# Folding an attention block's output projection into a router and the first expert matrices, and running a split matmul as one contraction

## The reference

```python
def _forward(hs, q_w, ..., o_w, o_b, router_w, router_b, w1, b1, w2, b2):
    Q = (hs @ q_w + q_b).reshape(B, S, H, HD).transpose(0, 2, 1, 3)        # H = 16
    K = (hs @ k_w + k_b).reshape(B, S, H, KPH).transpose(0, 2, 1, 3)       # KPH = 4
    V = (hs @ v_w + v_b).reshape(B, S, H, KPH).transpose(0, 2, 1, 3)
    scores = jnp.einsum('bhsk,bhtk->bhst', Q[..., :KPH], K) / math.sqrt(KPH)
    ao = jnp.einsum('bhst,bhtv->bhsv', jax.nn.softmax(scores, axis=-1), V)
    ao = ao.transpose(0, 2, 1, 3).reshape(B, S, H * KPH)                   # 64 features
    ao = jnp.concatenate([ao, jnp.zeros((B, S, D - LAT))], axis=-1)
    mla_out = ao @ o_w + o_b
    probs = jax.nn.softmax(mla_out @ router_w + router_b, axis=-1)
    topw, topi = jax.lax.top_k(probs, 2)
    combine = ...                                                          # 8 weights per token
    h1 = jnp.einsum('bsd,edf->ebsf', mla_out, w1) + b1[:, None, None, :]   # 8 experts, 256 wide
    h1 = jax.nn.gelu(h1, approximate=False)
    h2 = jnp.einsum('ebsf,efd->ebsd', h1, w2) + b2[:, None, None, :]
    return hs + 0.3 * jnp.einsum('bse,ebsd->bsd', combine, h2)

x = x + _L0_xattn_ref(_layernorm(x), ctx_1024)      # attention over 77 context rows
x = x + _L0_ffn_ref(_layernorm(x), ...)             # the block above
x = x + _L1_xattn_ref(_layernorm(x), ctx_1024, ...) # a second one over the context
x = x + _L1_ffn_ref(_layernorm(x), ...)             # one expert of 512
```

## Time and profile before

| | us |
|---|---|
| median of 3 runs | 174.09 |
| lowest and highest | 173.69, 174.84 |
| profiled execution | 173.32 |
| its span in the profile | 171.5 |
| PE busy in the span | 156.5 |
| mean granted clock of PE | 0.988 |

### The profile page before, as it was taken

One profiled execution on the slowest core, in us unless ns is written; L12 is line 12 of the kernel. 1 busy time (PEld: TensorE's weight loads), 2 busy tenths in 40 slices (PEclk: granted clock), 3 DMA queues, 4 the chain that ended last, 5 costly groups with the idle time before them and its releaser, 6 DMA issues.

```text
span 171.5 us, 4032 instructions
## 1 busy us (share of the span) xinstructions
PE 156.5 (91%) x1358; PEld 127.3 (74%) x1366; DVE 107.4 (63%) x401; ACT 106.5 (62%) x234; POOL 41.5 (24%) x122
## 2 busy tenths in 40 slices
...
GB/s 111 126 13 258 234 26 71 94 25 160 135 196 70 4 0 4 0 4 2 2 4 0 0 0 0 4 0 0 4 2 0 0 4 2 0 4 0 0 63 61
DMA packets 10527, 7.21 MB, mean 42 GB/s; under 512 B 1596, under 2 KB 9868, under 8 KB 10508
## 3 DMA queue, kind: packets, MB, share of 16 engines
...
## 4 chain that ended last, share of the span: by engine, by line
issue 53%; PE 22%; DVE 10%; POOL 5%; DMA 3%; ACT 3%; SPq 1%; ACTq 1%; POOLq 1%; DVEq 0%
PE ps L1012 20%; DVE nmax L820 4%; DMA qbd<-scratch_q 3%; POOL rstd L534 2%; DVE qbd L814 2%; POOL xn L528 2%; PE ps L1034 1%; DVE res L789 1%; DVE part L792 1%; DVE part L789 1%; SPq L383 1%; ACTq L55 1%; ACT part L601 1%; SPq L384 1%; ACT pexp L620 1%
## 5 line engine op out<-in xcount | busy, mean ns | idle before, releaser
L657 ACT ACTIVATE vpad<-ps,cols 128x256 f32<-128x256 f32 (+1 forms) x48 | 23.9, 543 | 23.8 <-PE ps L1012 23.7
L1012 PE MATMUL ps<-w2s,vpad 128*128 128x128 f32 x256 | 32.1, 277 | 0.0
L1012 PEld LDWEIGHTS ps<-w2s,vpad 128*128 128x128 f32 x256 | 30.3, 192 | 0.6 <-issue 0.2
L909 DVE SCALAR_TENSOR_TENSOR vpad<-ps,comb,vpad 128x128 f32<-128x128 f32 x64 | 18.6, 343 | 15.5 <-PE ps L1012 15.5
L820 DVE TENSOR_REDUCE nmax<-ps 128x4 f32<-128x512 f32 x32 | 21.0, 685 | 4.1 <-PE ps L1012 4.1
L620 ACT ACTIVATE pexp<-ps 128x512 f32<-128x512 f32 x32 | 18.6, 597 | 5.5 <-PE ps L1012 3.5
L1012 PE MATMUL ps<-mla_hi,w_lo 128*128 128x256 f32 (+1 forms) x48 | 17.7, 370 | 0.2 <-ACT vpad L657 0.2
L1012 PE MATMUL ps<-kst,qbd 128*128 128x128 bf16 x128 | 12.1, 225 | 5.0 <-DVE qbd L814 2.4
L1012 PEld LDWEIGHTS ps<-kst,qbd 128*128 128x128 bf16 x128 | 8.4, 101 | 10.0 <-issue 7.9
L528 POOL TENSOR_TENSOR xn<-vpad,bqv 128x256 f32<-128x256 f32 (+1 forms) x3 | 2.7, 909 | 53.0 <-DVE vpad L909 53.0
L1012 PE MATMUL ps<-mla_hi,w_hi 128*128 128x256 f32 (+1 forms) x48 | 15.3, 319 | 0.0
...
## 6 DMA issues: line engine op xcount, KB each, us to landing
...
```

Of the source, the lines that this page charges most:

```text
L657: act.activation(hT[:, k % 2, c, 0:n], ps[:, h1_bank(k, c), 0:n], ACT.Gelu, bias=cols[:, e * F0 + c:e * F0 + c + 1]).then_inc(s["gelu_ok"], 1)
L909: dve.scalar_tensor_tensor(out=x2[:, a + i, :], in0=ps[:, 2 + k % 2, i * D:(i + 1) * D], scalar=comb[:, a + i, e:e + 1], in1=x2[:, a + i, ...
L1012: return nc.tensor.matmul(dst, lhsT, rhs, start=start, stop=stop)
```

## The change

`oproj` goes. The output weights are transposed on PE once (`oT`: ACT writes `woT`, each lane of 32 rows holding 16 rows of -wo and 16 of +wo) and multiplied into the router weights (`fr`: `rwo`, `rbo`) and into `w1` of each expert (`fold:e`: one 256-wide fp32 matmul and two of one column for the bias, copied back by ACT over `w1s`; `fb` adds the biases on DVE). POOL's split of `w1` now waits for its fold. `den` is two matmuls: `selnum` brings the numerators into both halves of each lane, so that `aoT` holds the attention output twice per lane. ACT rounds it to `ao_hi`, and DVE forms `ao2`, which is -high in the rows of the negative weights and the low part in the others (`ao2 = aoT * lower - ao_hi`). With that, `m1` needs two matmuls per chunk instead of three. `comb_T` uses a transpose, one record, in place of an fp32 matmul with the identity. `wo` comes by one transfer of 64 rows instead of four. Several semaphores are merged. In bank 4, `fold`, `oT` and `fr` take turns with `den` and the router. The whole text of the order is rewritten; of its 35 lines the first is shown. The warm-up matmuls are 35 instead of 54.

```diff
-        wo = sb("wo", [P, D])
-        mla_hi = sb("mla_hi", [D, NHALF, T], FP32R)
-        mla_lo = sb("mla_lo", [D, NHALF, T], FP32R)
+        wo = sb("wo", [LAT, D])
+        woT = sb("woT", [D, LANES, 2, GROUPS, KPH])
+        lower = sb("lower", [P, 1])
+        ao_hi = sb("ao_hi", [D, NHALF, T], FP32R)
+        ao2 = sb("ao2", [D, NHALF, T], FP32R)
...
-        w1s = sb("w1s", [D, E0, F0 * P])
+        w1s = sb("w1s", [P, E0, F0 * P + F0])
...
-            warm:13 a_v:0 selg z_mask p1_stats:0 p1_norm:0 z_sel:0 z_v:0 warm:4 a_v:1 p1_ctx:0 warm:1 p1_T:0 warm:5 p1_stats:1
+            warm:1 selg a_v:0 warm:1 a_v:1 warm:1 z_mask warm:4 z_v:0 warm:5 z_q:0 z_den warm:2 p1_stats:0 a_q:0 warm:1 p1_norm:0
...
             def split_w1(e):
-                if e == 0:
-                    pool.wait_ge(s["w1_in"], 48)
-                a = did(pool.tensor_copy(w1_hi[:, e, :], w1s[:, e, :]))
-                after(a)
-                pool.tensor_tensor(out=w1_lo[:, e, :], in0=w1s[:, e, :], in1=w1_hi[:, e, :].bitcast(FP32),
+                w = w1s[:, e, 0:F0 * P]
+                pool.wait_ge(s["w1o_ok"], e + 1)
+                a = did(pool.tensor_copy(w1_hi[:, e, :], w))
+                after(a)
+                pool.tensor_tensor(out=w1_lo[:, e, :], in0=w, in1=w1_hi[:, e, :].bitcast(FP32),
                                    op=ALU.subtract).then_inc(s["w1_split"], 1)
...
-            def oproj(h):
-                act.wait_ge(s["o_ps"], h + 1)
-                act.activation(mlaT[:, h, :], ps[:, 4, :], ACT.Identity, bias=cols[:, R_OB:R_OB + 1]).then_inc(s["mla_ok"], 1)
-                act.wait_ge(s["mla_ok"], h + 1)
-                act.activation(mla_hi[:, h, :], mlaT[:, h, :], ACT.Copy).then_inc(s["mlahi_ok"], 1)
+            def high_part(h):
+                act.wait_ge(s["ao_ok"], HALF * (h + 1))
+                act.activation(ao_hi[:, h, :], aoT[:, h, :], ACT.Copy).then_inc(s["aohi_ok"], 1)
+
+            def wo_T():
+                act.wait_ge(s["woT_ps"], 1)
+                v = ps[:, 4, 0:LAT].rearrange("p (g j v) -> p j g v", g=GROUPS, v=KPH)
+                act.activation(woT[:, :, 0], v, ACT.Copy, scale=-1.0)
+                act.activation(woT[:, :, 1], v, ACT.Copy).then_inc(s["woT_ok"], 1)
+
+            def fold(e):
+                act.wait_ge(s["w1o_ps"], e + 1)
+                act.activation(w1s[:, e, :], ps[:, 4, 0:F0 * P + F0], ACT.Copy).then_inc(s["w1o_ok"], 1)
...
-                                   bias=cols[:, e * F0 + c:e * F0 + c + 1]).then_inc(s["gelu_ok"], 1)
+                                   bias=b1o[:, e, c:c + 1]).then_inc(s["gelu_ok"], 1)
...
-                dve.tensor_tensor(out=aoT[:, h, i * S:(i + 1) * S], in0=un[:, b % 2, :], in1=rden[:, b % 2, :],
+                dve.tensor_tensor(out=aoT[:, h, i * S:(i + 1) * S], in0=ps[:, 4, S:2 * S], in1=rden[:, b % 2, :],
                                   op=ALU.mult).then_inc(s["ao_ok"], 1)
 
-            def oproj(h):
-                dve.wait_ge(s["mlahi_ok"], h + 1)
-                dve.tensor_tensor(out=mla_lo[:, h, :], in0=mlaT[:, h, :], in1=mla_hi[:, h, :].bitcast(FP32),
-                                  op=ALU.subtract).then_inc(s["mlalo_ok"], 1)
+            def low_part(h):
+
+                dve.wait_ge(s["aohi_ok"], h + 1)
+                dve.wait_ge(s["obs_ok"], 2)
+                dve.scalar_tensor_tensor(out=ao2[:, h, :], in0=aoT[:, h, :], scalar=lower[:, 0:1], in1=ao_hi[:, h, :].bitcast(FP32),
+                                         op0=ALU.mult, op1=ALU.subtract).then_inc(s["ao2_ok"], 1)
+
+            def wo_T():
+                dve.wait_ge(s["cols_ok"], 1)
+                dve.tensor_scalar(obs[:, :], ones[:, :], cols[:, R_OB:R_OB + 1], None, ALU.mult).then_inc(s["obs_ok"], 1)
+                dve.wait_ge(s["ident_ok"], 1)
+                dve.tensor_reduce(lower[:, :], ident[:, :].rearrange("p (j x) -> p j x", j=LANES)[:, :, 16:32], axis=AX.XY,
+                                  op=ALU.add).then_inc(s["obs_ok"], 1)
+
+            def router_fold():
+
+                dve.wait_ge(s["rwo_ps"], 1)
+                dve.wait_ge(s["obs_ok"], 2)
+                dve.tensor_scalar(rwo[:, :], ps[:, 4, 0:E0], lower[:, 0:1], None, ALU.mult)
+                dve.tensor_tensor(out=rbo[:, :], in0=ps[:, 4, E0:2 * E0], in1=rb[:, :], op=ALU.add).then_inc(s["rwo_ok"], 1)
+
+            def bias_fold():
+                dve.wait_ge(s["w1o_ok"], E0)
+                dve.wait_ge(s["cols_ok"], 1)
+                dve.tensor_tensor(out=b1o[:, :, :], in0=w1s[:, :, F0 * P:F0 * P + F0],
+                                  in1=cols[:, 0:E0 * F0].rearrange("p (e c) -> p e c", c=F0), op=ALU.add).then_inc(s["b1o_ok"], 1)
...
-                pe.wait_ge(s["ln_ok"] if b else s["part_ok"], b or NFRONT)
-                if b >= HALF:
-                    pe.wait_ge(s["mla_ok"], 1)
-                if b >= HALF + 1:
+                pe.wait_ge(s["ao_ok"] if b else s["rwo_ok"], b or 1)
+                if 1 <= b <= HALF:
+                    pe.wait_ge(s["w1o_ok"], 2 * b)
+                elif b > HALF:
                     pe.wait_ge(s["lg_sub"], 1)
-                mm(ps[:, 4, 0:S], selden[:, :], un[:, b % 2, :]).then_inc(s["den_ps"], 1)
-
-            def oproj(h):
-                pe.wait_ge(s["ao_ok"], HALF * (h + 1))
-                pe.wait_ge(s["ow_in"], 16 * LANES)
-                mm(ps[:, 4, :], wo[:, :], aoT[:, h, :]).then_inc(s["o_ps"], 1)
+                mm(ps[:, 4, 0:S], selden[:, :], un[:, b % 2, :])
+                mm(ps[:, 4, S:2 * S], selnum[:, :], un[:, b % 2, :]).then_inc(s["den_ps"], 1)
+
+            def wo_T():
+                pe.wait_ge(s["w1_in"], 64)
+                pe.wait_ge(s["part_ok"], NFRONT)
+                nc.tensor.transpose(ps[:, 4, 0:LAT], wo[:, :], ident[0:LAT, 0:LAT]).then_inc(s["woT_ps"], 1)
+
+            def router_fold():
+
+                pe.wait_ge(s["woT_ok"], 1)
+                pe.wait_ge(s["obs_ok"], 1)
+                mm(ps[:, 4, 0:E0], woT[:, :, :, :, :].rearrange("p j a g v -> p (j a g v)"), rw[:, :])
+                mm(ps[:, 4, E0:2 * E0], obs[:, :], rw[:, :]).then_inc(s["rwo_ps"], 1)
+
+            def fold(e):
+
+                if e % 2:
+                    pe.wait_ge(s["w1o_ok"], e)
+                else:
+                    pe.wait_ge(s["ao_ok"], e // 2 + 1)
+                n = F0 * P
+                mm(ps[:, 4, 0:n], woT[:, :, :, :, :].rearrange("p j a g v -> p (j a g v)"), w1s[:, e, 0:n])
+                for c in range(F0):
+                    last = mm(ps[:, 4, n + c:n + c + 1], w1s[:, e, c * P:(c + 1) * P], cols[:, R_OB:R_OB + 1])
+                last.then_inc(s["w1o_ps"], 1)
 
             def router(h):
-                pe.wait_ge(s["mla_ok"], h + 1)
-                if h == 0:
-                    pe.wait_ge(s["ln_ok"], HALF + 1)
-                pe.wait_ge(s["w1_in"], 48)
+                pe.wait_ge(s["ao_ok"], BATCH if h else HALF + 1)
                 for n in range(HALF):
-                    last = mm(ps[:, 4, n * E0:(n + 1) * E0], mlaT[:, h, n * S:(n + 1) * S], rw[:, :])
+                    last = mm(ps[:, 4, n * E0:(n + 1) * E0], aoT[:, h, n * S:(n + 1) * S], rwo[:, :])
...
-                    last = mm(ps[0:E0, (7, 4)[h], n * S:(n + 1) * S], comb[:, h * HALF + n, :], ident[:, :])
+                    last = nc.tensor.transpose(ps[0:E0, (7, 4)[h], n * S:(n + 1) * S], comb[:, h * HALF + n, :], ident[:, :])
...
-                split3(ps[:, h1_bank(k, c), 0:n], w1_hi[:, e, f], w1_lo[:, e, f], x4_hi[:, toks(u)], x4_lo[:, toks(u)]).then_inc(s["h1_ps"], 1)
+                dst, x = ps[:, h1_bank(k, c), 0:n], ao2[:, :, :].rearrange("p h t -> p (h t)")[:, toks(u)]
+                mm(dst, w1_lo[:, e, f], x, True, False)
+                mm(dst, w1_hi[:, e, f], x, False, True).then_inc(s["h1_ps"], 1)
```

More of the change, by code:

```diff
@@ L100, in build @@
         aoT = sb("aoT", [P, NHALF, T])
-        mlaT = sb("mlaT", [D, NHALF, T])
+        own = sb("own", [P, NHALF, T])
         VB = GROUPS * LANES * ROWS
@@ L297, in build @@
-            s2:6,1 s2:6,2 un:5 av:5,3 w1:3 av:6,0 p4_ctx:0 combine:0 mT:7 s2:6,3 den:5 p4_ctx:1 s2:7,0 s2:7,1 msp:4 av:6,1 av:6,2
-            norm:4 norm:5 un:6 av:6,3 cT:0 av:7,0 s2:7,2 norm:6 s2:7,3 msp:5 norm:7 den:6 b2:0 av:7,1 av:7,2 w1:4 un:7 av:7,3
-            m1:0,0,0 msp:6 den:7 x2_init:0 gelu:0,0 m1:0,0,1 m1:0,1,0 oproj:1 m1:0,1,1 m1:0,2,0 gelu:0,1 gelu:0,2 m1:0,2,1
-            router:1 gelu:0,3 m2:0,0 m2:0,1 m1:0,3,0 m1:0,3,1 acc:0,0 m1:0,4,0 m2:0,2 gelu:0,4 gelu:0,5 acc:0,1 m1:0,4,1 cT:1 w1:5
```

118 lines of the change are left out of this document (62 added, 56 removed).

## The result

The changed kernel takes 167.54 us in the median of four runs (167.11 to 168.65), the kernel before 173.89 beside it; the ratio is 0.9637 with an interval of 0.9576 to 0.9699. Medians here are of all runs, while a ratio leaves out runs more than 1.5% above the fastest of their kernel. The profiled execution took 167.53 us for its span of 165.7.

The account below looks back on a forecast made before the run. PE's matmuls bound the kernel after 60 us, the query reload and DVE's maxima before. -5.1 + 0.8 + 0.5 = -3.8, plus 0.2 makes -3.6: 169.7 profiled, 170.5 us median, range 166.5 to 174.8.

Parts of the forecast that it names:

- 1.6 hidden: Between score groups of batches 4 and 5: 1.6 us of PE's added work is covered beside DVE's maxima.
- The third matmul, 7.4 us, of which 0.8 is lost: Expert stage: dropping each `m1` chunk's third matmul saves PE 7.4 us; 0.8 of 8 is charged for DVE or latency.
- The work that comes before the first `m1`: Behind the reload: five folds (4.25 us), `selnum` (1.2) and moved softmax and `av` groups (1.1), together 6.55 on PE.
- Before the reload, +0.5: Ahead of the second half's first score group: PE's extra 2.35 us delays it by up to 1 us, costing 0.5.
- 0.2 us charged for `msp:6`: POOL's maxima split for batch 6 queues behind `w1` splits and may be up to 1 us late; 0.2 added.
- Warm-up matmuls at nothing: Front: fewer warm-ups may bring a second half-clock window, but DVE binds there; 0 to 1 us, taken as 0.
- Rival B: Folds cost their whole 6.8 us and DVE or the PE-gelu chain binds late: -1.0, 173 us; chance 0.25.
- Rival D: Attention: PSUM bank 4, shared by `den`, folds, router and `oT`, sets the pace: +2, 176.1 us; chance 0.14.
- its own sign of more than 7 us between two `den` calls: Attention: if bank 4 sets the pace, the changed profile shows `den` calls more than 7 us apart.
- its other sign: Attention: if bank 4 sets the pace, PE idles before a `den` or a fold, released by ACT's copy.
- Rival C: Everything added is covered, by openings before the reload and maxima after it; only removals count: -6.5, 167.6 us; chance 0.15.

Follow-up runs that it names:

- a_three: The changed kernel with a third matmul put back into every `m1` chunk; 175.14 us, ratio 1.0071 to the kernel before.
- b_two: The kernel before with one of three matmuls per `m1` chunk left out, in the old order; ratio 0.9814 to the kernel before.
- b_aq3: The kernel before with ACT's zeroing of the last query tile moved earlier in the order; 174.04 us, ratio 1.0006.
- b_aq3w1: The kernel before with ACT's zeroing earlier and POOL's first `w1` split behind the maxima's split of sequence 2; 172.90 us, ratio 0.9943.
- a_again: The changed kernel run once more, unaltered, on the same chip as a repeat with more warm-up matmuls; 168.04 us.
- b_two_ct: The kernel before with two matmuls per `m1` chunk and the second half's combine-weight transpose moved behind `m1:0,5,1`; 170.33 us, ratio 0.9806.
- a_nofold: The changed kernel with all eight folds of `w1`, ACT's copies and their waits left out; 167.25 us, ratio 0.9554.

## Why the prediction was nearly right, and where it was not

The forecast was 170.5, the result 167.54, inside the range (166.5 to 174.8) but with a gain of 6.3 us where I had 3.6. In the profiled executions it is 5.8 (173.32 to 167.53); 0.6 more comes from the kernel before, whose profile was one of its shorter runs. The time fell in the range, and PE's busy time fell by 3.6 us (2.5 to 4 forecast), but the other sizes that the prediction names for the trace mostly did not come out: first score group of sequence 4 at 50.58 (51.3 to 52 forecast), first `m1` at 78.11 (79 to 80.5), from there 7.4 less (8). These forecasts did not agree among themselves either: 3 later and 8 less make -5, while the sum has -3.8. By the sum's own terms, reload to first `m1` was to grow by 6.55 less 1.35 (`oproj:0`, `cT:0`) less 1.6 hidden, 3.6, and the rest to shrink by 8.75 - 0.8 = 7.95.

- *The third matmul, 7.4 us, of which 0.8 is lost.* Right: 6.8 us in the stretch of `m1` and 6.6 in the profiled time (a_three). What I did not see is that this is so in the new order and not in the old one, where about 3 us come (b_two). The profile of before shows DVE's combine weights ready just as PE asked for them; that they would be late with less work ahead could have been read there.
- *The work that comes before the first `m1`.* A fold of 0.85 was right (0.85 to 0.92), as were the 128x1 records (0.11, against 0.10). The prediction has no term for two steps that changed places with the first `m1`: `b2:0` (eight records, 0.9 us) went behind it, and `den:7` (0.2) ahead of it. With them PE's added work between reload and first `m1` is 4.5 us, of which +2.25 shows, so that some 2.2 us lie in openings where I had 1.6; behind the first `m1` 8.05 us less was due and 7.37 came, so that 0.7 was lost where I charged 0.8. The mis-sized term is what is hidden: leaving the folds out gives back only 1.1 of 4.3 us.
- *Before the reload, +0.5.* This step failed: it is -0.70 in this pair. I had looked at PE's extra work alone, and called SP's and POOL's order neutral. The reload's first transfer starts a microsecond earlier (42.06, before 43.08), because the ACT step that released it before now stands earlier in ACT's order and because POOL's first split of `w1` no longer runs beside DVE's last split (b_aq3, b_aq3w1). Both rows stood in the old trace: SP released by ACT at 43.03, and 1.14 us for a 512-wide DVE step of which two 256-wide ones take 0.42 each. With its 1.2 us this is the largest part of the 2.2 us between forecast and profile. The size is that of one pair: other traces of the new order with as much half clock in the front put the first score group at 50.53 and 51.43 (a_three, a_again), of the old one at 51.73 and 51.89 (b_two_ct, b_two).
- *The rest:* 0.2 us charged for `msp:6` did not occur.
- *Warm-up matmuls at nothing.* Not contradicted: adding some back shortened the spans by about as much in either kernel and gained no time in the new one.
- *Rival B* falls: PE waits nowhere between reload and first `m1`, and in 120 to 150 it is busy for 9.7, 9.3 and 9.6 of 10, not under 9.0. *Rival D* falls, but not by its own sign of more than 7 us between two `den` calls. The calls from 40.63 on stand 6.0, 6.1, 5.8 and 8.3 us apart; here is the last pair, and under it the call of before whose successor stands 7.6 later:

```profile
58.53 0.38 PE L1046 MATMUL ps<-un,selden 128*128 128x128 f32 x2
66.85 0.38 PE L1046 MATMUL ps<-un,selden 128*128 128x128 f32 x2
```

```profile
55.99 0.44 PE L1012 MATMUL ps<-un,selden 128*128 128x128 f32 x2
```

The mean of the four is 6.6 where I had 5.8, and the 5.2 of before hid gaps from 3.2 to 7.6. Without any fold the long gap is still 7.9 (a_nofold), so that the folds do not make it. D falls because its other sign is missing: PE waits for no copy of ACT there. A longer turn costs 0.5 us.

*Rival C* gave the right number (167.6) by luck. It has the whole gain behind the reload, where 5.1 us came, and nothing ahead of it. Its cover holds in part: the folds ahead of the reload are covered, those after it not wholly.
